# The hardware loop over the expert tiles written out on three engines

## What is computed

```python
# layer 0: h is (8, 256, 128), 8 experts, the best 2 per token
gate_logits = xs @ Wg
weights, sel = jax.lax.top_k(gate_logits, 2)
weights = softmax(weights)
h = relu(einsum('td,edf->etf', xs, W1) + b1[:, None, :])     # F = 512
out_e = einsum('etf,efd->etd', h, W2) + b2[:, None, :]
out = einsum('tk,tkd->td', weights, out_e[sel, tok[:, None]])
# layer 1: the same shapes, with a gate and an up matrix
h = silu(einsum('bth,fh->btf', x, gw)) * einsum('bth,fh->btf', x, uw)
y = einsum('btf,hf->bth', h, dw)
```

## Time and profile before

| | |
|---|---|
| median of 3 runs | 704.83 us (703.49 to 705.87) |
| span of the profiled execution | 747.2 us (no other time is given for it) |
| mean granted TensorE clock | 0.811 of full |
| TensorE busy (matmuls / weight loads) | 503.5 us / 401.7 us |
| VectorE busy | 386.2 us |
| ScalarE busy | 262.4 us |
| GpSimd busy | 337.1 us |

### The profile page before, as it was taken

How to read it: one execution, slowest core, us unless ns; L and a number is a source line. 1 busy time by engine, 2 the same in 40 slices (tenths; PEclk the granted TensorE clock), 3 DMA queues, 4 the chain that set the end, 5 groups by cost and what they waited for, 6 DMA issues and landing times.

```text
span 747.2 us, 13354 instructions
## 1 busy us (share of the span) xinstructions
PE 503.5 (67%) x4221; PEld 401.7 (54%) x4221; DVE 386.2 (52%) x996; ACT 262.4 (35%) x639; POOL 337.1 (45%) x425
## 2 busy tenths in 40 slices
PE   6384878563277687773369977969831678878870
PEld 5263655452177586762346555545420578878770
DVE  5373977464934344444487554644227534434335
ACT  1221223111044334432125543535600455545442
POOL 2731545233156555654324432636731355555543
PEclk9686878765578979895589988989955699999995
DMA  6667564612011111112564545432221011111116
GB/s 187 148 177 151 138 165 139 158 35 63 1 36 44 39 35 42 39 40 86 160 159 101 111 112 99 124 81 50 60 53 36 22 39 36 39 38 36 35 33 168
DMA packets 67649, 61.94 MB, mean 83 GB/s; under 512 B 9792, under 2 KB 59456, under 8 KB 66048
## 3 DMA queue, kind: packets, MB, share of 16 engines
q1 hardware_dynamic: 50128, 40.05, 21.4%
q10 hardware_dynamic: 12480, 11.04, 5.4%
q0 software_dynamic: 4992, 10.23, 4.5%
HBM read 44.19 MB, written 17.10 MB: 82 GB/s over the span
## 4 chain that ended last, share of the span: by engine, by line
PE 34%; DMA 16%; issue 12%; DVE 12%; SPq 8%; another core or an unknown queue 6%; POOL 5%; ACT 4%; ACTq 1%; DVEq 1%; POOLq 0%
PE bank L797 11%; PE pair L808 6%; DMA max_d<-qk 5%; DMA stack_k<-parts_d 4%; PE pair L797 3%; SPq L454 2%; DMA parts_d<-parts 2%; SPq L433 2%; PE bank L875 2%; PE bank L604 2%; SPq L438 2%; PE pair L861 1%; DMA probs<-h_d,src_row 1%; PE pair L841 1%
## 5 line engine op out<-in xcount | busy, mean ns | idle before, releaser
L797 PE MATMUL bank<-probs,stack_q 128*128 128x128 f32 x708 | 103.7, 296 | 41.8 <-ACT probs L1443 21.0
L1669 POOL DMA_INDIRECT ye_d<-probs,dst_row x78 | 78.3, 1004 | 95.9 <-DVE probs L1217 45.3
L797 PEld LDWEIGHTS bank<-probs,stack_q 128*128 128x128 f32 x708 | 93.2, 207 | 48.9 <-issue 22.7
L1663 POOL DMA_INDIRECT probs<-h_d,src_row x78 | 75.9, 974 | 38.3 <-issue 20.4
L808 PE MATMUL pair<-qk,stack_k 128*128 128x128 f32 x624 | 89.8, 290 | 3.3 <-DVE stack_k L1225 3.1
L808 PEld LDWEIGHTS pair<-qk,stack_k 128*128 128x128 f32 x624 | 81.8, 204 | 6.4 <-issue 5.8
L1717 POOL TENSOR_SCALAR_AFFINE_SELECT probs<-probs 128x256 f32<-128x256 f32 (+1 forms) x96 | 46.4, 487 | 76.3 <-ACT probs L1534 75.7
L1534 ACT ACTIVATE probs<-pair 128x512 f32<-128x512 f32 x96 | 56.6, 598 | 50.0 <-PE pair L861 49.3
L1204 DVE COPY qk<-W 128x512 f32 x78 | 37.4, 479 | 49.2 <-issue 26.3
L875 PE MATMUL bank<-probs,V 128*32 128x256 f32 (+1 forms) x512 | 52.0, 337 | 4.1 <-POOL probs L1717 3.9
L841 PE MATMUL pair<-stack_k,stack_q 96*128 96x128 bf16 (+1 forms) x256 | 41.7, 273 | 17.8 <-DMA stack_k<-parts_d 11.1
(11 more groups left out here) (194 smaller groups left out, 992.7 us busy)
## 6 DMA issues: line engine op xcount, KB each, us to landing
parts_d<-parts SPq DMA_DIRECT2D x16, 384.0 KB, 3.9
W<-in_w ACTq DMA_DIRECT2D x16, 256.0 KB, 3.8
stack_q<-parts_d SPq DMA_DIRECT2D x16, 192.0 KB
stack_k<-parts_d SPq DMA_DIRECT2D x16, 192.0 KB
mod_bc<-mod_d SPq DMA_DIRECT2D x16, 192.0 KB, 6.0
W_up<-in_up_w ACTq DMA_DIRECT2D x8, 256.0 KB, 4.6
stack_q<-parts_d SPq DMA_DIRECT2D x16, 128.0 KB
stack_k<-parts_d SPq DMA_DIRECT2D x16, 128.0 KB
```

What stands on the lines that cost most here:

```text
L797: i = pe.matmul(at[r % 2][:, k * P:(k + 1) * P], w_now[:, r % 2, which, k * P:(k + 1) * P], x_t[:, r % 2, :], start=True, stop=True)
L1663: gp.indirect_dma_start(out=x_rows[:, n % RING, :], out_offset=None, in_=h_d[l], in_offset=bass.IndirectOffsetOnAxis(ap=src_row[:, n:n + 1 ...
L1669: gp.indirect_dma_start(out=ye_d[l], out_offset=bass.IndirectOffsetOnAxis(ap=dst_row[:, n:n + 1], axis=0), in_=y_rows[:, n % RING, :], in_ ...
```

## The change

The hardware loop goes. `all_tiles` now emits all 39 tiles one after the other in every engine's stream, with constants for buffer numbers, semaphore values and the place in `tile_exp`. `exists` and `at_least` lose the case of a register. The expert number is still loaded at run time for each tile. The other engines' code, the tiles' order and all data movement stay as they are. Seven lines are fewer, so line n behind the helpers is line n - 7 in the changed kernel.

```diff
-PEEL = TILES % RING + RING
-TURNS = (TILES - PEEL) // RING - 1
...
 def exists(n):
-    return not isinstance(n, int) or 0 <= n < TILES
+    return 0 <= n < TILES
...
-def all_tiles(eng, step):
-    for n in range(PEEL):
-        step(n, n % RING, n // RING)
-    with eng.Fori(0, TURNS) as i:
-        for u in range(PEEL, PEEL + RING):
-            step(i * RING + u, u % RING, i + u // RING)
-    for n in range(TILES - RING, TILES):
+def all_tiles(step):
+    for n in range(TILES):
         step(n, n % RING, n // RING)
...
 def at_least(eng, sem, count, base=0):
-    if not isinstance(count, int) or count > 0:
+    if count > 0:
         eng.wait_ge(sem, count + base)
...
-                all_tiles(pe, step)
+                all_tiles(step)
...
-                all_tiles(ve, step)
+                all_tiles(step)
...
-                all_tiles(act, step)
+                all_tiles(step)
```

## The result

The changed kernel takes 707.66 us (median of 20 runs, 702.67 to 711.04) against 703.52 us for the kernel before (20 runs, 699.13 to 708.07) in the same comparison. The ratio is 1.0064, interval 1.0043 to 1.0086. So it is slower by about 4.1 us, and beyond the 2.1 us that the prediction called no change.

A forecast was written before the change was run, and what follows sets the result against it. GpSimd's queue was taken to bound layer 0's tiles and TensorE layer 1's. Branch 0.0, VectorE -0.3, TensorE and ScalarE 0.0, code 0.0 took the median from 704.83 to 704.5 us; range for 8 in 10: 699 to 710 us.

The forecast's parts named there:

- no change: Whole kernel: the median moves by no more than 2.1 us (0.3%); chance 0.63.
- The pace of the stages: Expert tiles: GpSimd's 2.57 us a tile bounds layer 0, TensorE's 2.79 us bounds layer 1.
- the branch is hidden: Tile loops: TensorE's branches lie under matmuls already queued, worth 0.0 us; 3.0 us if that cover were gone.
- TensorE's and ScalarE's waits are worth 0: Tile loops: replacing register waits by plain waits on these two engines gains 0.0 us.
- The stops: Expert tiles: late semaphores after TensorE's matmuls, 42.6 us of the chain, taken to belong to the profiled execution only.
- The first rival: Expert tiles: the stops are real and belong to the loop; without them 28.1 us faster, 676.7 us; chance 0.05.
- VectorE -0.3: Layer 0's tiles: simpler waits save VectorE 0.08 us a tile, mostly hidden under GpSimd; value 0 to -0.5 us.
- The change touches two stages only: Whole kernel: only the 39 expert tiles of layer 0 and of layer 1 are affected.
- code 0.0: Expert tiles: loads of the added code are hidden, 0 us; exposed they would cost 11.5 us.
- The third rival: Expert tiles: code arrives late, slower; 716.3 us fully exposed, 707.1 us with a fifth of it; chance 0.12.
- Saved refetches: Tile loops, fourth rival: 12 taken branches of TensorE refetch code, 11.5 us saved, 693.3 us; chance 0.01.

The follow-up runs named there:

- e5: The kernel before, unchanged, one more trace at the upper level, where it takes 753.55 us: span 748.4 us, time 750.17 us.
- e9: The kernel before, unchanged, one trace at the lower level, where it takes 704.55 us: span 698.0 us, attention stage 228.0 us.
- e4: The changed kernel again, all three loops written out, against the kernel before at 753.55 us (upper level): ratio 0.9958.
- e2: The kernel before with only VectorE's and ScalarE's loops written out, TensorE keeping its own, at the upper level (before 746.33 us): ratio 0.9916.
- e12: The kernel before with 192 wait-only instructions on TensorE (96 and 96) at the start of layer 1's attention stage: ratio 1.0021.
- e17: Repeat of the kernel before with 192 wait-only instructions on TensorE, in another comparison: ratio 0.9976.
- e6: The kernel before with 134 wait-only instructions on TensorE and 16 on VectorE at the start of layer 1's attention stage: ratio 1.0009.
- e13: Repeat of the kernel before padded by 134 wait-only instructions on TensorE and 16 on VectorE, in another comparison: ratio 1.0077.
- e10: Control: the kernel before with 256 wait-only instructions on TensorE and 128 on VectorE, later instructions keeping their place in load blocks: ratio 1.0053.
- e16: The kernel before with 256 wait-only instructions on TensorE (128 and 128) and none on VectorE: ratio 1.0022.
- e3: The kernel before with all three loops written out in layer 0 only, at the upper level (before 746.33 us): ratio 0.9953.
- e11: The kernel before with 64 wait-only instructions on TensorE at the start of layer 1's attention stage: ratio 1.0055.

## Why the prediction was wrong

**The pace of the stages** was right. GpSimd's 2.57 us and TensorE's 2.79 us are the bounds of the two tile stages (97.7 and 106.0 us by the prediction, 96.5 and 104.4 measured in the kernel before at the lower level), and layer 1's 104.40 us is the same in both kernels. That the branch is hidden, and TensorE's and ScalarE's waits are worth 0, is shown there.

**The stops** were read wrongly. "The two numbers agree, so I take these stops to belong to the profiled execution" compared a profile at the upper level with timed runs at the lower. In e5 span and time agree with the stops in both, and in e9 both are without. The first rival was right that they are real, and wrong that they belong to the loop: e4, with no loop, has them. At that level the change gains 0.4%, and VectorE's and ScalarE's part alone 0.8% (e2).

**"VectorE -0.3"** has the wrong sign at the lower level. The 0.08 us a tile came out as forecast, but they are hidden under GpSimd, and the step took GpSimd's issue for a constant. It lasts 0.97 or 1.2 us by what VectorE does beside it, and with the shorter VectorE cycle 8 to 10 of 73 are long instead of 0 to 7. The term measured +1.1 us. That a long issue follows the begin of a weight copy, and that the stage follows the issues, is shown; why the new phase of the engines meets more gathers is only argued, from the timelines. The Trainium skill, page "SBUF — State Buffer", section "SBUF: two separate sides", has a rule that bears on it: an f32 copy from SBUF to SBUF on VectorE locks the port pair that it shares with GpSimd, which then can't write the descriptors of its DMAs. Lines 1197 and 1200 are such copies, and the trace agrees in kind, though the gather loses 0.24 us and not the 0.65 us of both copies. I had not weighed this rule, and it spoke against the change.

**"The change touches two stages only", and with it "code 0.0",** is the step that failed. I looked for instruction loads in the tile stages, where TensorE waits for its own code, and found them hidden; they are. The third rival named the other way, a packet ahead of a data transfer, but looked for it at a gather. The larger part of the loss lies in layer 1's attention stage, which the change does not touch and the sum did not contain: 231.3 us in the mean of the four traces written out at the lower level, against 228.7 us for the old code, +2.6 us where the sum had nothing. With layer 0's +1.1 us that makes 3.7 of the 4.1 us; the rest is within the scatter. That the stage is longer is shown, with TensorE's loop alone written out (e1), with VectorE's and ScalarE's (e2), and at both levels. That shifted loads are the reason is supported by the padded copies and not proven, as said below.

The measured 707.66 us lies within the stated 699 to 710 us, and near the third rival's 707.1 us for a fifth of the loads exposed. Both are luck: the upper part of the range stood for loads exposed in the tile stages, and none is exposed there.

The Trainium skill, page "Runtime: NRT & Kernel Launch", section "Instruction fetch mechanics", gives a code fetch after a taken branch, where the target lies outside the window of the instruction memory, as a reason to unroll. Saved refetches would have made the unrolled loop faster. The runs don't show it: layer 1's tile stage is equal to 0.1 us with and without branches. Whether this loop's targets lie outside the window was never shown, so nothing here speaks against the rule itself.

**What stays open.** Four things keep the loads from being the shown cause. First, time and trace disagree: e12 and e17 had long stages in their traces (232.6 and 231.5 us) and no loss in the mean of their two ratios (0.9999). Second, one kernel does not give one length: e6 and e13 are the same program, with its 16 KB packets within 5 us of the same places, and their stages took 233.0 and 229.6 us. Third, what the transfers of a trace take above their medians without a packet, summed, hardly follows the stage's length (correlation 0.24 over the 20 traces). Fourth, TensorE's granted clock was not held fixed. It is lower in the longer stages (correlation -0.55), though it does not decide alone: e5 took 229.0 us at 0.80, e6 233.0 us at 0.80. Padding in front costs 0.30% in the mean, a little over twice its standard error, and in e10 and e16 part of that is the padding's own delay; the changed kernel has no padding, so that part does not carry over to it. Nor is it known what sets the two levels.

## What to carry to other kernels

Unrolling a loop whose branch is already covered buys nothing at the bound, and it moves every later instruction load. Where a later stage waits for small transfers one after the other, read how long those take with a load beside them (here 1.4 against 2.2 to 2.5 us), and count that stage into the sum although no line of it changes. Before an effect is explained by comparing a span with timed runs, see that both stand at the same level. Below half a per cent compare the mean of several comparisons, not one ratio. And before padding is used as a control, measure what one instruction of it takes from start to start, and see that the gap holds it.

## What the runs showed of the hardware

An 8 KB instruction load during the last 16 KB den_d transfer went with 2.2 to 2.5 us in all eight traces that had one, against 1.4 us in the twelve without, though the load itself is one packet of 0.3 to 0.6 us. It is not so for every transfer: beside the den_d before it a 16 KB load left 1.42 us in e1, e3 and e4, and went with 3.02 us in e11. A GpSimd gather issue of 0.97 us took up to 1.22 us when VectorE's f32 copy began 0.05 to 0.18 us ahead of it, and a VectorE copy that began within a gather took 0.60 instead of 0.43 us in the case shown above. 128 wait-only instructions took 13.6 us on TensorE's sequencer (e10). The same program took 703 to 705 us in some comparisons and 746 to 754 us in others, with a granted clock of 0.80 to 0.83 in both; the difference is in pieces of 1.4 to 5.5 us in the expert tiles, which the chain calls "another core or an unknown queue".
